# Sums of squares of the last 40 k and q units, taken as one fp32 product or as two fp32r products of a high and a low part

## The reference, cut to what matters

```python
ada = silu(c) @ Wada.T + bada                 # six vectors of 512 per batch
h = rmsnorm(x, g1) * (1 + scale_msa) + shift_msa
q, k, v = split(h @ Wqkv.T + bqkv)            # 16 heads of 32
q = rmsnorm(q, gq) * 32 ** -0.5               # norm over the 32 of one head
k = rmsnorm(k, gk)
o = softmax(q @ k.T) @ v
x = x + gate_msa * (o @ Wproj.T + bproj)
x = x + gate_mlp * (gelu(modulated rmsnorm(x) @ Wfc1.T + bfc1) @ Wfc2.T + bfc2)
```

## Time and profile before

| | us |
|---|---|
| median of 3 runs | 1779.41 (1778.92 to 1780.18) |
| the profiled execution, its own time | 1781.35 |
| its span in the profile | 1779.2 |
| busy: TensorE, VectorE, ScalarE, GpSimd | 1727.3, 1061.8, 926.4, 367.0 |
| steps 104 to 111, length | 28.1 |
| steps 176 to 207, length of eight | 27.3, 27.4, 27.7, 26.7 |

### The profile page before, as it was taken

One profiled execution on the slowest core, in us unless ns is written; L12 is line 12 of the kernel. 1 busy time (PEld: TensorE's weight loads), 2 busy tenths in 40 slices (PEclk: granted clock), 3 DMA queues, 4 the chain that ended last, 5 costly groups with the idle time before them and its releaser, 6 DMA issues.

```text
span 1779.2 us, 23361 instructions
## 1 busy us (share of the span) xinstructions
PE 1727.3 (97%) x8436; PEld 1154.4 (65%) x8436; DVE 1061.8 (60%) x1301; ACT 926.4 (52%) x1160; POOL 367.0 (21%) x303
## 2 busy tenths in 40 slices
PE   7999999999999999999999999999999999999999
PEld 4555555555555555554334787888888888888887
DVE  5678887889898988878787444142332324141311
ACT  4577776777777777778887432222222222222221
POOL 2001110100001000000140233333333333333332
PEclk8999999999999999999999999999999999999999
DMA  7555555555655555555765201010020202010000
GB/s 278 139 133 147 137 141 139 126 149 139 158 136 129 149 132 147 127 149 144 180 154 199 75 19 57 27 52 26 11 72 6 65 18 63 20 53 24 13 23 24
DMA packets 122243, 176.92 MB, mean 99 GB/s; under 512 B 29569, under 2 KB 43905, under 8 KB 121137
## 3 DMA queue, kind: packets, MB, share of 16 engines
q1 hardware_dynamic: 119648, 163.75, 34.5%
q10 hardware_dynamic: 1712, 9.47, 1.4%
q0 software_dynamic: 800, 2.62, 0.5%
HBM read 124.87 MB, written 50.92 MB: 99 GB/s over the span
## 4 chain that ended last, share of the span: by engine, by line
PE 79%; DVE 10%; ACT 6%; issue 4%; DMA 1%; POOL 0%; SPq 0%; ACTq 0%; DVEq 0%
PE scores L1387 19%; PE pv L1404 10%; PE gemm L1404 10%; PE scores L539 10%; PE pv L556 9%; PE gemm L620 7%; ACT probs L748 4%; DVE sums L833 4%; PE pv L1359 4%; PE gemm L633 4%; PE aux L586 2%; PE aux L573 1%; DVE raw L858 1%; DVE raw L910 1%; PE aux L1374 1%
## 5 line engine op out<-in xcount | busy, mean ns | idle before, releaser
L748 ACT ACTIVATE probs<-scores,shift 128x1024 f32<-128x1024 f32 x512 | 549.4, 1114 | 185.6 <-PE scores L539 177.7
L833 DVE TENSOR_TENSOR sums<-sums,probs 128x2048 f32<-128x2048 f32 x186 | 440.3, 2367 | 30.4 <-ACT probs L748 25.4
L539 PE MATMUL scores<-q_stack,k_stack 128*128 128x512 f32 x1024 | 356.9, 433 | 6.9 <-ACT probs L748 5.7
L1387 PE MATMUL scores<-w_hi,act_parts 128*128 128x512 f32 x1016 | 316.4, 393 | 0.0
L539 PEld LDWEIGHTS scores<-q_stack,k_stack 128*128 128x128 f32 x1024 | 172.5, 188 | 200.8 <-issue 107.0
L1319 POOL TENSOR_TENSOR act_parts<-act_full,act_parts 128x512 fp32r<-128x512 f32 x127 | 170.6, 1343 | 477.7 <-ACT act_parts L1250 477.7
L556 PE MATMUL pv<-probs,v 128*32 128x512 f32 x2048 | 251.7, 600 | 0.4 <-ACT probs L748 0.4
L1387 PEld LDWEIGHTS scores<-w_hi,act_parts 128*128 128x128 f32 x1016 | 189.9, 189 | 38.7
L1387 PE MATMUL scores<-w_lo,act_parts 128*128 128x512 f32 x508 | 198.4, 390 | 0.0
L1463 DVE TENSOR_TENSOR y_next<-pv,p_bias 128x512 f32<-128x512 f32 x28 | 19.3, 691 | 298.6 <-PE pv L1359 298.6
L1250 ACT ACTIVATE act_parts<-act_full 128x512 fp32r<-128x512 f32 x127 | 80.3, 632 | 221.3 <-PE scores L1387 220.4
(11 more groups left out here) (187 smaller groups left out, 1951.2 us busy)
## 6 DMA issues: line engine op xcount, KB each, us to landing
k_stack<-parts_scratch SPq DMA_DIRECT2D x128, 256.0 KB, 4.9
q_stack<-parts_scratch SPq DMA_DIRECT2D x128, 256.0 KB, 5.0
parts_scratch<-parts SPq DMA_DIRECT2D x62, 512.0 KB, 3.0
inverse<-inverse_scratch SPq DMA_DIRECT2D x128, 64.0 KB, 2.1
heads_out<-o_out SPq DMA_DIRECT2D x32, 256.0 KB, 5.2
out<-result SPq DMA_DIRECT2D x30, 256.0 KB, 2.0
heads<-heads_out SPq DMA_DIRECT2D x28, 256.0 KB, 3.8
x_tile<-in_x SPq DMA_DIRECT2D x28, 256.0 KB, 2.7
```

Source lines behind the costliest of these rows:

```text
L539: mm = nc.tensor.matmul(scores[p][:, i, :], k_stack[s][:, h, j * P:(j + 1) * P], q_stack[half][:, h, :], start=True, stop=True)
L748: nc.scalar.activation(probs[L % RING][:, 2 * p:2 * p + 2, :], scores[p][:], ACT.Exp, bias=small["shift"][:]).then_inc(exp_done, 1)
L833: nc.vector.tensor_tensor(sums[:], a[:], probs[l % RING][:], ALU.add).then_inc(added, 1)
L1387: mm = nc.tensor.matmul(acc[t], parts_of(c, m)[:, b, t * P:(t + 1) * P], w2[a][:, m, :], start=(m == 0 and i == 0), stop=(m == NM - 1 and ...
```

## The change

The sums of squares of units 24 to 63 (40 units, `n >= HALVED`) are made in another way, and the tables move with them.

- ScalarE still writes the squares in fp32, and behind them writes them once more, rounded to fp32r (`squares_hi`).
- VectorE subtracts the rounded squares from the full ones, in place, into fp32r (`square_low`, placed two steps behind the unit's last, behind the add and ahead of `make_parts`).
- TensorE multiplies `head_ones` (now fp32r) with both, one product behind the other into the same bank, in step E+3 instead of E+2. The logarithm, inverse root, parts and the store of a unit follow one step later; for units 31, 47 and 63 the sum's step stays what it was, and for unit 25 it goes from 56 to 59.
- `squares_hi` lies where the third `xt` buffer was. From x tile 16 on, two buffers are used in turn, and a tile is loaded behind the transpose of the tile two earlier.
- `make_parts` is cut into functions that issue the same three instructions on the same engine. Units 0 to 23 keep the fp32 product, with `head_ones` read as fp32.

```diff
+def x_home(n):
+    return n % XS if n < 2 * NT else n % 2
+def x_owner(n):
+    if n < 2 * NT:
+        return n - XS
+    return 4 * NT - 1 - n if n < 2 * NT + 2 else n - 2
+XLOAD_AT = {TURN[x_owner(n)] + 1: n for n in range(NT + XS, B * NT)}
...
+HALVED = 6 * NU
 SUM_AT = {}
 for n, step in enumerate(UNIT_END):
-    step += 1 if step < 0 else 2
+    step += 1 if step < 0 else 2 if n < HALVED else 3
     while step in SUM_AT or step in ROWS_AT or step in TURN_AT and step >= 0:
         step += 1
     SUM_AT[step] = n
+SQ_LOW_AT = {step + 2: n for n, step in enumerate(UNIT_END) if n >= HALVED}
...
         def sum_squares(n):
...
+            else:
+                pe.wait_ge(sq_lo_done, n - HALVED + 1)
+                aux_free()
+                nc.tensor.matmul(aux[:], small["head_ones"][:], squares_hi[:], start=True, stop=False)
+                nc.tensor.matmul(aux[:], small["head_ones"][:], squares_lo[:], start=False, stop=True).then_inc(ss_mm, 1)
...
             nc.scalar.activation(squares[:], raw[n % 2][:], ACT.Square).then_inc(sq_done, 1)
+            if n >= HALVED:
+                if n == HALVED:
+                    act.wait_ge(turned, 2 * NT - 1)
+                nc.scalar.activation(squares_hi[:], raw[n % 2][:], ACT.Square).then_inc(sq_hi_done, 1)
...
+        def square_low(n):
+            dve.wait_ge(sq_done, n + 1)
+            dve.wait_ge(sq_hi_done, n - HALVED + 1)
+            nc.vector.tensor_tensor(squares_lo[:], squares[:], full(squares_hi[:]), ALU.subtract).then_inc(sq_lo_done, 1)
...
             if L > 0:
                 add(L - 1)
+            if L in SQ_LOW_AT:
+                square_low(SQ_LOW_AT[L])
             if L in FIN_AT and not parts_first:
                 make_parts(FIN_AT[L])
...
     put("squares", b + 4 * K, [CH])
+    put("squares_lo", b + 4 * K, [CH], F32R)
+    put("squares_hi", b + 16 * K, [CH], F32R)
```

More of the change, by code:

```diff
@@ L125 @@
 HOUT_AT = {step: n for n, step in enumerate(HOUT) if n not in HOUT_ACT.values()}
-XLOAD_AT = {step + 1: n + XS for n, step in enumerate(TURN) if NT <= n < B * NT - XS}
+def x_home(n):
[5 more added lines that the diff above has]
+XLOAD_AT = {TURN[x_owner(n)] + 1: n for n in range(NT + XS, B * NT)}
 XLOAD_AT.update({NT + n: NT + n for n in range(XS)})
@@ L235, in gpsimd @@
         pool.memset(ident[:], 0.0).then_inc(zeroed, 1)
-        pool.memset(bones[:], 0.0).then_inc(zeroed, 1)
+        pool.memset(full(bones[:]), 0.0).then_inc(zeroed, 1)
         pool.memset(small["ones"][:], 1.0).then_inc(masks, 1)
@@ L247, in gpsimd @@
             pool.wait_ge(masks, 5 + h)
-            pool.memset(bones[r, r], 1.0).then_inc(masks, 1)
+            pool.memset(full(bones[r, r]), 1.0).then_inc(masks, 1)
         pool.wait_ge(masks, 5 + HG)
@@ L344, in build_attention @@
     raw, squares, norms, parts, inverse, compact, o_out = (mem[x] for x in ("raw", "squares", "norms", "parts", "inverse", "compact", "o_out"))
+    squares_hi, squares_lo = mem["squares_hi"], mem["squares_lo"]
     xt, unused, h_full, v_bias, qk_bias, mod, scale1 = (mem[x] for x in ("xt", "unused", "h_full", "v_bias", "qk_bias", "mod", "scale1"))
@@ L360, in build_attention @@
     unit_mm, raw_done, sq_done = sem("unit_mm"), sem("raw_done"), sem("sq_done")
+    sq_hi_done, sq_lo_done = sem("sq_hi_done"), sem("sq_lo_done")
     ss_mm, ln_done, norm_done = sem("ss_mm"), sem("ln_done"), sem("norm_done")
@@ L384, in x_of @@
     def x_of(n):
-        return xt[n % XS] if n < XS or n >= NT else mem["x_ahead"][n - XS]
+        return xt[x_home(n)] if n < XS or n >= NT else mem["x_ahead"][n - XS]
     x_ahead_in = [sem(f"x_ahead_in{n}") for n in range(NT)]
@@ L392, in x_landed @@
             return x_ahead_in[n], 16
-        return x_in[n % XS], 16 * sum(1 for m in range(NT, n + 1) if m % XS == n % XS)
+        return x_in[x_home(n)], 16 * sum(1 for m in range(NT, n + 1) if x_home(m) == x_home(n))
     def parts_of(n):
@@ L418, in load_x @@
             if n >= NT:
-                sp.wait_ge(turned, n - XS + 1)
+                sp.wait_ge(turned, x_owner(n) + 1)
             b, t = n // NT, n % NT
@@ L583, in sum_squares @@
         def sum_squares(n):
-            pe.wait_ge(sq_done, n + 1)
-            aux_free()
-            nc.tensor.matmul(aux[:], small["head_ones"][:], squares[:], start=True, stop=True).then_inc(ss_mm, 1)
+            if n < HALVED:
+                pe.wait_ge(sq_done, n + 1)
+                aux_free()
+                nc.tensor.matmul(aux[:], full(small["head_ones"][:]), squares[:], start=True, stop=True).then_inc(ss_mm, 1)
+            else:
+                pe.wait_ge(sq_lo_done, n - HALVED + 1)
+                aux_free()
+                nc.tensor.matmul(aux[:], small["head_ones"][:], squares_hi[:], start=True, stop=False)
+                nc.tensor.matmul(aux[:], small["head_ones"][:], squares_lo[:], start=False, stop=True).then_inc(ss_mm, 1)
             issued["squares"] += 1
@@ L905, in split_low, with unit_norm @@
             nc.vector.tensor_tensor(h_lo[:, :, c], buffer_of_turn(n)[:], full(h_hi[:, :, c]), ALU.subtract).then_inc(lo_done, 1)
-        def make_parts(n):
+        def unit_norm(n):
             r = raw[n % 2]
@@ L910, in make_parts, with low_part @@
             nc.vector.scalar_tensor_tensor(r[:], norms[:], 1.0 / EPS2 ** 0.5, r[:], ALU.min, ALU.mult).then_inc(normed, 1)
+        def low_part(n):
+            gain = small["s_gain"][:] if UNIT[n][2] == "q" else 1.0
+            dve.wait_ge(part_hi, n + 1)
+            nc.vector.scalar_tensor_tensor(parts_of(n)[:, 1, :], raw[n % 2][:], gain, full(parts_of(n)[:, 0, :]), ALU.mult, ALU.subtract).then_inc(part_lo, 1)
+        def make_parts(n):
+            unit_norm(n)
             dve.wait_ge(normed, n + 1)
@@ L918, in make_parts @@
             gain = small["s_gain"][:] if UNIT[n][2] == "q" else 1.0
-            nc.vector.tensor_scalar(parts_of(n)[:, 0, :], r[:], gain, None, ALU.mult).then_inc(part_hi, 1)
-            dve.wait_ge(part_hi, n + 1)
-            nc.vector.scalar_tensor_tensor(parts_of(n)[:, 1, :], r[:], gain, full(parts_of(n)[:, 0, :]), ALU.mult, ALU.subtract).then_inc(part_lo, 1)
+            nc.vector.tensor_scalar(parts_of(n)[:, 0, :], raw[n % 2][:], gain, None, ALU.mult).then_inc(part_hi, 1)
+            low_part(n)
+        def square_low(n):
+            dve.wait_ge(sq_done, n + 1)
+            dve.wait_ge(sq_hi_done, n - HALVED + 1)
+            nc.vector.tensor_tensor(squares_lo[:], squares[:], full(squares_hi[:]), ALU.subtract).then_inc(sq_lo_done, 1)
         setup["vector_first"](dve)
@@ L1725, in program @@
                            ("silu", KT * B), ("x_gain", 1), ("y_gain", 1), ("s_gain", 1)):
-            small[name] = ctx.enter_context(nc.sbuf_tensor(name, [P, cols], F32))
+            small[name] = ctx.enter_context(nc.sbuf_tensor(name, [P, cols], F32R if name == "head_ones" else F32))
         mem = place(nc)
```

## The result

The changed kernel takes **1793.38 us** (median of 4 runs, 1792.67 to 1794.2), the kernel before 1779.47 us: ratio 1.0075, 95% interval 1.0063 to 1.0087, 13.9 us slower. The forecast was 1780.3 us, inside the noise of no change. The time is above the prediction's range, which ended at 1790.0 us.

The account below looks back on a forecast made before the run. TensorE, 97% busy with 79% of the chain, was taken as the bound, with VectorE near its end in the blocks. Group terms 2.4 - 0.3 - 0.3 - 0.9 = +0.9 us on 1779.41 gave 1780.3 us; range 1771 to 1790.

Parts of the forecast that it names:

- count of the waits at the bank: VectorE's low squares and parts meeting ahead of bank releases, where TensorE waits; priced group by group, +0.9 us in sum.
- TensorE's saving: Two fp32r products replace one fp32 product in 40 sums: 0.42 us each, 16.8 us at most.
- The block of eight steps: Units 32 to 39 and 48 to 55: low squares delay `v_out`; each of 8 blocks +0.3 us, +2.4 us in all.
- Units 56 and 57: In steps 176 to 210: said to have the block's form, +0.3 us together.
- units 40 and 41: In steps 112 to 146: same order of products as units 56 to 63, that group put at -0.3 us.
- Unit 60: Near step 197: add, low squares and unit 59's parts stand ahead of `v_out`, so TensorE starts later, +1.5 us.
- Units 24 to 31: 3.4 us saved, less waits of 1.8 us at unit 26 and 0.7 us at unit 27: -0.9 us.
- The low squares' own price: 40 VectorE subtractions at 688 ns, 27.5 us in all, about 0.65 us each from the queue; 1.3 us per block.
- Rival 2: VectorE sets the block's length: each grows by the added 1.38 us, 11.0 us over eight; 1791.4 us, chance 0.27.
- blocks over 29 us: Sign of VectorE setting the pace: blocks come out over 29 us with VectorE's idle gone.
- The lock: VectorE and GpSimd exclude each other on SBUF; low squares wait up to 1.29 us more; rival at 1788.0 us, chance 0.07.
- Nothing for x tiles, SP's queue and ScalarE: Two x buffers, SP's later store and ScalarE's 40 added squares cost nothing; x tiles up to 3 us once if held.

Follow-up runs that it names:

- shift_only: Kernel before, with only the sums of squares, logarithm, root, parts and store of units 24 to 63 one step later; no work added: 1792.62 us, +13.5 us.
- long_product: Changed kernel with one fp32 product of the high squares instead of two fp32r; low squares made and waited for, not summed: 1807.1 us, +28.0 us against the kernel before.
- no_low_late: Changed kernel without low squares, one fp32r product of the high squares, sums still in step E+3: 1771.74 us, -7.4 us against the kernel before.
- no_low_early: Changed kernel without low squares, one fp32r product of the high squares, sums back in step E+2: 1761.73 us, -17.4 us against the kernel before.
- low_unused: no_low_early plus low squares made in step E+2, left out of the sum, waited for only by ScalarE's next square: 1777.65 us, -3.1 us against the kernel before.
- shift_behind: shift_only with the parts of 27 units made right behind the move out of the bank instead of ahead: 1789.48 us, +9.6 us against the kernel before.
- even_early: Changed kernel with all sums in step E+2, new sums only for the 22 units summed in even steps, others fp32: 1805.44 us, +24.7 us against the kernel before.

## Why the prediction was wrong

The measured prices, each a difference of two runs: the later step +13.5 us (shift_only), the low squares with the second square beside them +14.5 us (long_product less shift_only), the shorter product -14.1 us (changed kernel less long_product). They sum to the 13.9 us by their making; what tests them is the second pair for the first two: the later step +10.0 us (no_low_late less no_low_early), the low squares +14.3 us (low_unused less no_low_early).

The same differences by stretches, from the traces, show that the three don't act in one place (us):

| steps | later step | low and second squares | shorter product | together | predicted |
|---|---|---|---|---|---|
| 48 to 79 | +3.4 | +1.4 | -1.8 | +3.0 | -0.9 |
| 80 to 111 and 144 to 175, the eight blocks | +1.3 | +8.3 | -4.6 | +5.0 | +2.4 |
| 112 to 143 | +4.2 | +1.2 | -2.4 | +3.0 | -0.3 |
| 176 to 207 | +3.1 | +2.2 | -2.5 | +2.9 | -0.3 |
| together | +12.0 | +13.0 | -11.2 | +13.8 | +0.9 |

A fall of the clock in shift_only (step 53) and one in long_product (step 147), 1.6 us each, are taken out; they are told in the last section. The second pairs give 10.9 us for the later step and 15.1 us for the low squares, counted in the same way over all four stretches. The low squares cost most in the blocks, the later step nearly all outside them.

The step of the prediction that failed is its count of the waits at the bank. Its +0.9 us is a saving of 16.8 us against 17.7 us of added waits; the runs show 14.1 us against 28.0 us, and TensorE's waits for moves out of the bank alone are 24.5 us longer. Term by term:

- **TensorE's saving, 16.8 us**: right as a size, 14.1 us came through (11.2 us in the stretches of the traces).
- **The block of eight steps, +0.3 us**: right for six of the eight. Blocks 88 to 111 and 152 to 175 are 0.41 to 0.47 us longer, by the mechanism named: `v_out` behind low squares and parts, then TensorE's wait (1.07 us at 509.45 us), then the line exponential, add, parts, move out. This I had laid out instruction by instruction. The first blocks, 80 to 87 and 144 to 151, have another order and are 1.2 us longer each; they were priced as the others.
- **Units 56 and 57 "have the block's form, +0.3 together"**: this term failed by the most, and with it the same sentence for units 40 and 41. A block's +0.3 us is a balance: +1.5 us at the v tile, where the sum of the unit before has come in too, then -0.3 us in the pair at 106, and -0.9 us in the pair at 110, which its own sum leaves. There are ten such v tiles (steps 88 to 120 and 152 to 184) for eight blocks. The last ones, at 120 and 184, bring +1.84 us in the pair, and no whole block pays it back. For the pairs from 176 to 184 the sum is +1.51 + 0.46 - 0.16 - 0.85 + 1.84 = +2.8 us, for those from 112 to 120 it is +2.3 us: 5.1 us where I had 0.6. That is 4.5 of the 12.9 us by which the stretches exceed my sum.
- **Unit 60, +1.5 us**: right in mechanism, with a wait of 1.16 us for the v tile; the pairs at 196 and 198 are 1.1 us longer together.
- **Units 24 to 31, -0.9 us**: wrong, +2.96 us, another 3.9 of the 12.9 us. I had taken two waits, for units 26 and 27, and they are there (1.20 and 0.72 us). Two more are there that the sum had not, for the moves of units 25 and 28, in steps 55 and 69; before, TensorE waits under 0.3 us at either.

```profile
298.82 0.50 PE L657 MATMUL gemm<-wq_hi,h_hi 128*128 128x512 f32 x1 [1.39 <-DVE raw L886]
...
352.58 0.50 PE L657 MATMUL gemm<-wq_hi,h_hi 128*128 128x512 f32 x1 [1.32 <-DVE raw L886]
```

Both are mostly the low squares' doing: in shift_only, which has none, they are 0.39 us each. The second low square is one of the ten that the lock holds:

```profile
350.07 1.79 DVE L961 TENSOR_TENSOR squares_lo<-squares,squares_hi 128x512 fp32r<-128x512 f32 x1
```

- **The low squares' own price**: mis-sized. I charged them 1.3 us a block, most of it taken into idle time, and nothing elsewhere except 0.65 us ahead of one v tile. They cost about 14 us however they were placed, of which about 5 us lie outside the blocks. Rival 2 had this: VectorE's added work sets the time, 1791.4 us, 2 us from what came. Its mechanism is half of the truth, since the later step, which adds no work, costs 13.5 us by itself; that the number came near is luck. Its sign, blocks over 29 us, shows in two of the eight.
- **The lock**: it moved from the adds to the low squares as the text said it might. The two totals nearly cancel, but at step 69 it lengthens a wait of TensorE.
- **Nothing for x tiles, SP's queue and ScalarE**: right. VectorE's wait for an x tile is 8.2 us in all, in the set-up, as before (8.1 us), and no_low_early has ScalarE's second square without a cost in its blocks.

What stays open: why the later step costs 9.6 us even with the parts behind the bank's moves (shift_behind). By stretches that is +5.3 us in steps 48 to 79 (1.5 of it the clock at step 53), +2.9 in 112 to 143 and +1.0 in 176 to 207, and nearly nothing in the blocks. The waits at the bank moved rather than left: 15.4 us against 7.5 before, the longest now 2.29 us at step 69, where the unit's move stands behind two adds that take 5.59 us, and 1.30 us at step 77. How much of this is the parts, now ahead of the next move, and how much the lock on the adds was not separated.

Of all kernels run, no_low_early is the fastest, 17.4 us below the kernel before, but it leaves the low parts of the squares out. None whose sums use them beat the kernel before: the shorter product saves 0.4 us of TensorE and needs 0.65 us or more of VectorE, ahead of a move that TensorE waits for.

## What to carry to other kernels

Where two engines meet at one buffer, price an edit by what it puts ahead of each release of that buffer, and count the releases themselves, not the blocks that they happen to lie in; one well worked block doesn't stand for a stretch in which only the ends differ. A busy share is no guide to where this bites: VectorE is 91% busy in the blocks and 75% in steps 184 to 191, and both stretches lost time. A step moved later with no work added can cost as much as the work: test the moved table alone first. Work moved from a full engine to an idle one is no relief where their instructions shut each other out.

## What the runs showed of the hardware that I had not expected

A wait of TensorE can be followed by a slower clock, and then costs more than its length. In even_early TensorE waited 1.98 us for a low square, and the granted clock of the next stretch fell to about half, the 1.2 GHz level. Windows of that run (the columns of the earlier trace rows):

```profile
466.00:469.40 3.40, 1.45 (x7) 0.84 (x5) 3.40 (x3) 2.12 (x2) 2.83 (x1) 1.00 0.72 141
469.40:473.00 3.60, 3.57 (x9) 2.80 (x10) 2.28 (x2) 1.81 (x2) 0.00 (x0) 0.53 0.21 42
473.00:480.00 7.00, 7.00 (x39) 4.38 (x38) 6.24 (x6) 5.50 (x7) 0.00 (x0) 1.00 0.15 55
```

In the second of these the records of its products are 0.63 us long where they are 0.40 elsewhere, and the pair at 100 is 3.4 us longer than before, while the pair at 108, with a like wait but no drop, is 1.8 us longer. The run has seven such waits, of 1.96 to 1.98 us, and five of them are followed by a drop, some 1.6 us each, 8 of its 24.7 us.

A drop can also come or stay away behind the same wait. At step 53, ahead of all that shift_only changed, TensorE waits 2.58 us for a unit's move in the kernel before and in shift_only alike; the clock falls behind it in shift_only and not in the kernel before. Seven of the thirteen traces have this drop and six don't. That of long_product at step 147 follows a wait of 1.73 us. Windows of shift_only:

```profile
284.00:287.00 3.00, 0.67 (x3) 0.19 (x1) 2.36 (x4) 2.12 (x3) 0.00 (x0) 1.00 0.00 0
...
288.40:291.80 3.40, 3.40 (x17) 1.24 (x19) 2.89 (x2) 2.24 (x3) 0.00 (x0) 0.50 0.50 170
```

Its pair at 52 takes 11.94 us, that of the kernel before 10.38 us. So a trace can carry some 1.6 us that another with the same instructions does not, and stretches are compared only once such drops are looked for. The changed kernel has none in its attention steps, and the kernel before one, at step 13, outside of the stretches compared: this is no part of the 13.9 us that the stretches show.
